# Banded attention on one core: both score products in four 32-column strips, masks on diagonal blocks only

## What is computed

```python
dist = q_pos[:, :, None] - k_gpos[:, None, :]
allowed = (dist > 0) & (dist <= w) & (k_gpos[:, None, :] >= 0)     # w = 128
scores = einsum('bhnqd,bhnkd->bhnqk', qb, kb) * scale              # 16 heads, head width 8
attn = softmax(where(allowed, scores, NEG))
out = einsum('bhnqk,bhnkd->bhnqd', attn, vb)
```

## Time and profile before

| | |
|---|---|
| median of 3 runs | 614.55 us (608.69 to 614.93) |
| the profiled execution | 620.31 us, its span 618.6 us |
| PE busy | 571.3 us (92%), 5504 matmuls, 5509 weight loads |
| DVE, ACT, POOL busy | 448.0, 290.6, 344.9 us |
| granted TensorE clock, mean | 0.965 of full speed |
| instruction records in all | 17277 |

### The profile page before, as it was taken

The page is one execution under the profiler, slowest core; times in us unless marked ns, Lnnn a source line. Parts: engine busy times, 40 slices in busy tenths (PEclk is TensorE's granted clock), DMA queues, the critical chain, the costliest instruction groups (busy, mean ns, idle before and its releaser), DMA issues. The chain is left out here.

```text
span 618.6 us, 17277 instructions
## 1 busy us (share of the span) xinstructions
PE 571.3 (92%) x5504; PEld 390.2 (63%) x5509; DVE 448.0 (72%) x2031; ACT 290.6 (47%) x787; POOL 344.9 (56%) x749
## 2 busy tenths in 40 slices
PE   7898869979999999899999999987799999999992
PEld 3555336747777677577777777754367766776672
DVE  6884458838888888688888888885464767766646
ACT  1464305727676676567776767773132121212110
POOL 4664202637885878658888588898212242432251
PEclk9997979969999999899999999998999999999997
DMA  4586850633542454255433440000000000000001
GB/s 132 176 259 180 200 111 9 133 50 46 59 52 41 50 66 50 30 54 63 49 45 52 59 58 11 4 2 1 2 2 0 2 19 17 17 0 17 19 18 34
DMA packets 56590, 33.83 MB, mean 55 GB/s; under 512 B 5850, under 2 KB 55426, under 8 KB 56506
## 3 DMA queue, kind: packets, MB, share of 16 engines
q1 hardware_dynamic: 55450, 32.45, 29.0%
q10 hardware_dynamic: 1056, 0.35, 0.2%
HBM read 21.18 MB, written 11.27 MB: 52 GB/s over the span
## 5 line engine op out<-in xcount | busy, mean ns | idle before, releaser
L1036 DVE CUSTOM_DVE_ANT_0 added<-psS,maskq 128x256 bf16<-128x256 f32 x512 | 205.5, 412 | 61.1 <-PE psS L893 53.7
L1267 ACT ACTIVATE probs<-psST 128x512 f32<-128x512 f32 x256 | 154.0, 603 | 109.5 <-PE psST L914 108.3
L914 PE MATMUL psST<-qst,kst 98*128 98x128 bf16 x1024 | 101.7, 222 | 5.0 <-DMA qst<-mT 4.7
L914 PEld LDWEIGHTS psST<-qst,kst 98*128 98x128 bf16 x1024 | 79.1, 99 | 28.0 <-DMA qst<-mT 6.7
L893 PE MATMUL psS<-kst,qst 68*128 68x256 bf16 x448 | 88.6, 280 | 1.3 <-DVE rowmax L1036 0.8
L930 PE MATMUL psPV<-probs,vst 128*9 128x128 f32 x2048 | 82.2, 280 | 0.8 <-POOL probs L1182 0.4
L1179 POOL TENSOR_SCALAR_AFFINE_SELECT probs<-probs 128x256 f32<-128x256 f32 x140 | 57.9, 413 | 33.9 <-ACT probs L1267 33.7
L1700 ACT ACTIVATE hT<-fpsH 128x512 f32<-128x512 f32 x32 | 19.1, 598 | 121.6 <-PE fpsH L1444 121.6
L1182 POOL TENSOR_SCALAR_AFFINE_SELECT probs<-probs 128x256 f32<-128x256 f32 x140 | 57.4, 410 | 0.0
L893 PEld LDWEIGHTS psS<-kst,qst 68*128 68x128 bf16 x448 | 35.0, 102 | 33.7 <-issue 22.3
L1441 PE MATMUL fpsH<-xehi,w1hi 128*128 128x512 f32 x128 | 55.7, 435 | 0.0
(11 more groups left out here) (179 smaller groups left out, 1144.3 us busy)
## 6 DMA issues: line engine op xcount, KB each, us to landing
qst<-q_parts SPq DMA_DIRECT2D x96, 64.0 KB
kst<-k_parts SPq DMA_DIRECT2D x96, 64.0 KB
q_parts<-split SPq DMA_DIRECT2D x8, 384.0 KB, 2.7
k_parts<-split SPq DMA_DIRECT2D x8, 384.0 KB, 2.9
v_tok<-vt SPq DMA_DIRECT2D x8, 288.0 KB, 3.3
vst<-v_tok SPq DMA_DIRECT2D x16, 144.0 KB
X<-in_L_attn_x_dram SPq DMA_DIRECT2D x8, 256.0 KB, 3.0
out_dram<-res SPq DMA_DIRECT2D x8, 256.0 KB, 2.2
```

The costliest lines, as they stand in the source:

```text
L914: last = nc.tensor.matmul(bank[:, a, side * P:(side + 1) * P], kst[0:KALL, h, ring(n - 1 + side)], qst[0:KALL, h, ring(n)], start=not mask ...
L1036: taken = nc.vector.tensor_tensor_reduce(added[:, h], psS[g % 2][:, a], mask[:], 1.0, NEG * 4, ALU.add, ALU.max, rowmax[:, n.mod(2), h:h + 1])
L1267: nc.scalar.activation(probs[:, g], psST[g % 2][:].rearrange("p a c -> p (a c)"), ACT.Exp, scale=SCALE).then_inc(s_exp.sem, 1)
```

## The change

Both score products are cut into four strips of 32 columns of the array. In `scores` a strip is 32 queries as the stationary operand against the 160 keys of their band, so `psS` is filled 160 wide instead of 256, and each head takes 4 products instead of 1. `maskq` and `added` become 160 wide, and `maximum` reads 160 elements.

In `scores_t` a strip is 32 keys against the queries that may see them: 32, 64, 96 and 128 queries of the block before, and 128, 96, 64 and 32 of the own block. That is 8 products per head instead of 2. What is never written in a bank keeps a large negative number that DVE puts there once, ahead of the steps. Inside the 32 x 32 blocks on the diagonal the mask is still added, by four products of 128 columns per unit, now in all eight units of all steps, the first block of each sequence apart. So POOL's `select` and its tables go.

The loads of the masks are small pieces now: 16 transfers of 4 or 20 KB take the place of four that had 640, 512, 128 and 128 KB. They are in the list that SP issues early in `project`.

```diff
...
+                    for i in range(QUADS):
+                        q = qst[0:KPROD, h, part(n, QD * i, QD)]
+                        if n.mod(RING):
+                            last = nc.tensor.matmul(bank[quad(i), a, 0:WIN], q, kst[0:KPROD, h, part(n - 1, QD * i, WIN)],
+                                                    start=True, stop=True)
...
-                masked = n.mod(RING) == 0 or g not in SELECTED
-                if masked:
-                    which = n.over(RING, 1, 1) if n.mod(RING) == 0 else 0
-                    nc.tensor.matmul(bank[:], identb[:],
-                                     maskk[:, which, :].unsqueeze(1).broadcast_to([P, 2, 2 * P]),
-                                     start=True, stop=False)
+                first = n.mod(BB) == 0
+                for j in range(QUADS):
+                    pick = identb[:, quad(j)]
...
+                        nc.tensor.matmul(bank[quad(j)].rearrange("p a (s q) -> p a s q", s=2)[:, :, :, quad(j)], pick,
+                                         maskk[:].unsqueeze(1).broadcast_to([P, 2, 2, QD]),
+                                         start=True, stop=False, skip_group_check=True)
...
-                    for side in range(2):
-                        last = nc.tensor.matmul(bank[:, a, side * P:(side + 1) * P],
-                                                kst[0:KALL, h, ring(n - 1 + side)], qst[0:KALL, h, ring(n)],
-                                                start=not masked, stop=(not masked or (a == 1 and side == 1)))
+                    if not first:
+                        for j in range(QUADS):
+                            nc.tensor.matmul(bank[quad(j), a, 0:QD * (j + 1)], kst[0:KALL, h, part(n - 1, QD * j, QD)],
+                                             qst[0:KALL, h, part(n, 0, QD * (j + 1))],
+                                             start=False, stop=True, skip_group_check=True)
+                    for j in range(QUADS):
+                        last = nc.tensor.matmul(bank[quad(j), a, P + QD * j:2 * P], kst[0:KALL, h, part(n, QD * j, QD)],
+                                                qst[0:KALL, h, part(n, QD * j, P - QD * j)],
+                                                start=False, stop=True, skip_group_check=True)
...
-                cleared = [k + 1 for k, unit in enumerate(SELECTED) if unit // 2 == G]
-                if cleared:
-                    pe.wait_ge(s_sel.sem, s_sel.after(n, cleared[-1]))
...
+            nc.vector.memset(never[:], NEG).then_inc(s_consts, 1)
+            for bank in psST:
+                nc.vector.memset(bank[:], NEG).then_inc(s_consts, 1)
...
-                taken = nc.vector.tensor_tensor_reduce(added[:, h], psS[g % 2][:, a], mask[:], 1.0, NEG * 4,
+                taken = nc.vector.tensor_tensor_reduce(added[:, h], psS[g % 2][:, a, 0:WIN], mask, 1.0, NEG * 4,
...
-                    select(s, SELECTED[1])
-                    select(s, SELECTED[2])
-                    select(s, SELECTED[3])
```

More of the change, by code:

```diff
@@ L54 @@
 VW = HD + 1
+QD = 32
+QUADS = P // QD
+WIN = P + QD
 UN = H // 2
-SELECTED = (0, 2, 3, 4, 6)
 EPS = 1e-5
@@ L271, in sandwich @@
         for_attend = [
-            (held.maskk_f[:], c_maskk), (held.lat_row_f[:], c_latrow), (held.lat_col_f[:], c_latcol),
-            (held.maskq_tab[:], c_maskq[:, 1:]), (held.maskq[:], c_maskq[:, 0]), (held.maskq0[:], c_maskq[:, 1]),
+            *((held.maskk_f[quad(j), side], c_maskk[quad(j), 0, side * P + QD * j:side * P + QD * (j + 1)])
+              for side in range(2) for j in range(QUADS)),
+            (held.lat_row_f[:], c_latrow), (held.lat_col_f[:], c_latcol),
+            *((held.maskq[quad(i), which], c_maskq[quad(i), which, QD * i:QD * i + WIN])
+              for which in range(2) for i in range(QUADS)),
             (held.valid[:], c_valid), (held.wout[:], out_w), (held.bout[:], bcast_rows(out_b)),
@@ L839, in ring, with part @@
             return slice(n.mod(RING) * P, (n.mod(RING) + count) * P)
+        def part(n, first, count):
+            return slice(n.mod(RING) * P + first, n.mod(RING) * P + first + count)
         FIRST, LAST = -2, NB + 2
@@ L890, in scores @@
                     h = 2 * g + a
[L891 to L898, removed]
+                    for i in range(QUADS):
[3 more added lines that the diff above has]
+                                                    start=True, stop=True)
+                        else:
+                            nc.tensor.matmul(bank[quad(i), a, 0:P - QD * i], q,
+                                             kst[0:KPROD, h, part(n - 1, QD * i, P - QD * i)], start=True, stop=True)
+                            last = nc.tensor.matmul(bank[quad(i), a, P - QD * i:WIN], q,
+                                                    kst[0:KPROD, h, part(n, 0, QD * (i + 1))], start=True, stop=True)
                 last.then_inc(s_S.sem, 1)
@@ L911, in scores_t @@
+                if first:
+                    for j in range(QUADS):
+                        nc.tensor.matmul(bank[quad(j), :, P + QD * j:P + QD * (j + 1)], identb[:, quad(j)],
+                                         maskk[:, 1].unsqueeze(1).broadcast_to([P, 2, QD]),
+                                         start=False, stop=False, skip_group_check=True)
                 for a in range(2):
                     h = 2 * g + a
-                    for side in range(2):
-                        last = nc.tensor.matmul(bank[:, a, side * P:(side + 1) * P],
-                                                kst[0:KALL, h, ring(n - 1 + side)], qst[0:KALL, h, ring(n)],
-                                                start=not masked, stop=(not masked or (a == 1 and side == 1)))
+                    if not first:
[3 more added lines that the diff above has]
+                                             start=False, stop=True, skip_group_check=True)
+                    for j in range(QUADS):
+                        last = nc.tensor.matmul(bank[quad(j), a, P + QD * j:2 * P], kst[0:KALL, h, part(n, QD * j, QD)],
+                                                qst[0:KALL, h, part(n, QD * j, P - QD * j)],
+                                                start=False, stop=True, skip_group_check=True)
@@ L1166, in _ @@
             pool.wait_ge(s_consts, CONSTS)
-            pool.sem_inc(s_fill, 1)
-            def select(n, g):
-                if n.mod(RING) == 0:
-                    pool.sem_inc(s_sel.sem, 1)
-                    return
-                pool.wait_ge(s_exp.sem, s_exp.after(n, g + 1))
-                stand(pool, s_pass_pool)
-                before, own = (probs[:, g].rearrange("p (a side q) -> p a side q", a=2, side=2)[:, :, side]
-                               for side in range(2))
-                nc.gpsimd.affine_select(out=before, in_=before, compare_op=ALU.is_gt, fill=0.0, base=0,
-                                        pattern=[[0, 2], [1 - P, P]], channel_multiplier=P)
-                nc.gpsimd.affine_select(out=own, in_=own, compare_op=ALU.is_gt, fill=0.0, base=0,
-                                        pattern=[[0, 2], [1, P]], channel_multiplier=-1).then_inc(s_sel.sem, 1)
             def emit(s):
```

36 lines of the change are left out of this document (15 added, 21 removed).

## The result

The changed kernel took **636.84 us** (630.62 to 652.79), the kernel before 614.74: ratio 1.036, 95% interval 1.022 to 1.050, so slower. The direction and the mechanism of the forecast held, its size did not: +22 us where +108 was forecast. Some executions of any of these kernels take some per cent longer at a lower clock; a ratio with an interval compares the others, so it can differ from the ratio of the medians.

A forecast was written before the change was run, and what follows sets the result against it. PE was taken as the bound before, its instruction fetch after. Fetch +112, DVE -2 and constants +1.1 made +111 on the profiled 620.3 us; on 614.55 that is 725.6, rounded down to 722 us, range 590 to 790.

The forecast's parts named there:

- PE's work: PE's products in the steps: 0.38 us a unit for 0.52 to 0.54; a step of 9.6 us would become 8.3.
- DVE's maximum: Row maximum in `scores` over 160 for 256 elements: 0 to 2.5 us saved per step, hidden by PE; -2 us counted.
- POOL's selections: POOL's 280 selections of 0.41 us go; POOL is not waited for, so nothing is gained.
- Blocks wanted: PE's instruction blocks: 623 instructions a step for 277, 2.43 blocks; about 87 blocks and 1.4 MB on the instruction queue.
- The steps of 13.6 us: Sign that the forecast is right: steps of about 13.6 us, those without loads near 12.
- How fast blocks come: Instruction fetch in the steps: 4.9 us a block idle, 7 us under loads; 77 blocks in 435 us, +112 us.
- 11.6 us under loads: Longest time for a block while loads run, the upper end for the fetch term: given as +152 us.
- The clock: PE at half clock after stops: +25 us if a quarter of 51 blocks meet it; 0 in the sum, left to the range.
- The rule weighed: Skill's statements on PE's instruction store: 2048 instructions with crossings mostly hidden, against only two blocks, which the prediction's one stop fitted.
- A: Rival: instruction blocks come in time, the row-maximum transfer chain holds, -22 us, 592 us; chance 0.18.
- B: Rival: strips' weights load one after another on PE, +1.9 us per step, +61 us, 675 us; chance 0.07.
- C: Rival: no change to speak of, gain eaten by stops, a block every 3.9 us on average, 615 us; chance 0.05.

The follow-up runs named there:

- experiment 2: Changed kernel with only one product in strips, the other as before: `scores` alone 632.9 us (ratio 1.027), the transposed product alone 642.45 us (1.027).
- the two profiles: Two profiled executions of the same changed kernel, nothing altered between them: the first took 652.79 us, the second 631.75 us.
- experiment 4: Changed kernel without the loads' bytes, plus 8 one-column strip products with weight loads ahead of each unit's masks: 662.62 us (ratio 1.082).

## Why the prediction was right in sign and wrong in size

*PE's work: right.* 0.36 us a unit for the 0.38 forecast, a fed step of 8.5 us for 8.3. It rests on strips standing next to strips (experiment 2), which I had counted but not seen as a condition. DVE's maximum takes 0.32 us for the 0.3 named. That POOL's selections were free holds: with five of them back, and the masks' instructions gone, the kernel was 8 us faster.

*Blocks wanted: right.* 87 blocks and 1.43 MB, as forecast; stops put to issue, of 1 to 8 us, most of the long ones beside loads; PE at 87%. The steps of 13.6 us, named as a sign too, did not come (11.3 and 10.5 in the two profiles).

*How fast blocks come: the step that failed.* "With the DMA engines nearly idle, block to block took 4.9 us when PE was out of instructions" and "7 us" beside loads. Measured: 3.9 us idle (experiment 4) and 4.6 to 5.0 beside loads. 75 blocks x 4.36 = 327 us and x 4.67 = 350 us for the two profiles, where I had 77 blocks in 435. Both figures came from one event, in part at half clock (0.51 from 254.0 us), and the second was merely the middle between 4.9 and the longest time that had shown no stop. I gave 4.9 as the least that there could be; one event can't bound from below. Taken apart, its parts are those of experiment 4: landing at 251.2, PE on at 252.7, but the next fetch at 255.0, 2.3 us later instead of 1.4. (A slip besides: with 11.6 us under loads the prediction's sum gives +161, not +152. It bears only on the range.)

With the measured prices the same sum, 38 intervals away from loads at 3.9 and 37 beside them at 4.6, gives 318 us against 326.6 and 350.2 measured, and 318.8 for the kernel before. What lies above it I put to stretches at half clock, in which PE itself needs 6.1 us for a block (459 instructions in the 11 us of 380 to 391). The traces bear on that: intervals at full clock throughout are 4.1 us on average (44 of them) in the first profile and 4.2 (54) in the second, 4.3 of them beside loads and 3.9 to 4.0 away; those that touch half clock are 5.5 (30) and 4.9 (20). So the 4.6 beside loads holds some of the clock's part already. It stays argued which causes which, as a late block makes an interval long and lowers the clock too, and no run of the changed kernel kept the clock up with the loads in place.

*The clock: right to leave it in the range, wrong in its reason.* I expected regular gaps of 1.5 us with the clock whole. In the kernel with the one-column products it is so: stops of 0.8 to 2.2 us and a granted clock of 1.00 from 300 us on. In the changed kernel the few long stops bring the half clock (0.50 in 380 to 391). Intervals away from loads are 4.3 us in the first profile and 4.1 in the second instead of 3.9; that is 38 x 0.2 to 0.4 = 8 to 15 us, the part of it that can be seen apart from the loads.

*The rule weighed.* After a missing fetch PE stopped when one block's work was done, and a fetch started only once PE had begun on a block (experiment 4). The Trainium skill (Runtime: NRT & Kernel Launch, section Instruction fetch mechanics) has two statements: PE's store of 2048 instructions, with crossings mostly hidden, and a store of only two blocks. The runs go against the first: with the DMA engines nearly idle and about 3.2 us of work in a block, PE stood over 0.8 us at 41 of some 90 crossings, and a fetch of 1.1 to 1.2 us began only when PE was on the block before. They go with the second.

*The rivals.* A (blocks in time, 592) didn't happen. Its chain of row-maximum transfers was hardly met: PE waited for it 6.9 us in four steps of the first profile and 0.5 us in the second. Without the loads' bytes the supply still held the time at 605. B (weights of strips one after another) is refuted by the unit above. C had the time within 22 us, its reason being the right one in weaker form: "a block every 3.9 us on average" was its condition, and that turned out to be the idle supply.

## What to carry to other kernels

Count an engine's instructions before cutting its work into smaller ones: here a block of 256 came every 3.9 us with the DMA engines nearly idle and every 4.4 to 4.7 in steps with these loads, so a PE stream with more than 66 instructions per us (58 in such steps) is bound by their supply, and one that is close to it can absorb no delay. Where blocks last twice as long as the supply needs, spreading a burst of transfers over the steps is worth having: it gave the kernel before 1.6% with no change of its work. A price that rests on one event is a point, not a bound.

## What the runs showed of the hardware that I had not expected

- PE's instructions are fetched one block at a time, in a cycle: PE begins a block, 1.3 us later the next fetch starts, 1.1 to 1.2 us later it has landed, and 1.4 us after that PE can begin on it (means over the 41 stops of experiment 4; each part varies by some 0.3 us).
- Semaphore increments on PE are not free: 43 in a row stopped it for 0.11 us each and 16 in a row for 0.06, and the granted clock went down to 0.50 throughout the steps.
- Half of this change gives no faster fed step (9.9 and 9.6 us for 9.6) and the whole does (8.5), by two changes of width of 0.1 us a unit; with two strips of 64 columns a fed step is slower than at full width (10.0).
